# Sixteen-head attention before a transformer stream: one pipeline of four sequences in place of two passes of three stages

## The reference, cut to what matters

```python
x = x + attn_a(layernorm(x))          # changed part: x is 4 sequences x 512 tokens x 128, 16 heads of 8
x = x + ffn(layernorm(x))             # 2 layers of local attention + gated MLP
x = x + attn_b(layernorm(x))
x = x + ffn(layernorm(x))

def attn_a(x):
    q, k, v = split_heads(x @ w_qkv + b_qkv)                # (4, 16, 512, 8) each
    p = softmax(einsum('bhnd,bhmd->bhnm', q, k) * 8 ** -0.5)
    return merge_heads(einsum('bhnm,bhmd->bhnd', p, v)) @ w_proj + b_proj
```

## Time and profile before

| | |
|---|---|
| median of 3 runs | 1183.93 us (1179.61 to 1187.25) |
| profiled execution, its own time | 1180.76 us |
| its span, first to last instruction | 1179.0 us |
| busy in the span | TensorE 996.0, DVE 827.2, ACT 717.2, GpSimd 390.5 us |
| chain that ended last | TensorE 46%, DVE 13%, issue 4%, ACT 3%, GpSimd 2% |
| mean granted TensorE clock | 0.930 |

### The profile page before, as it was taken

How to read it: one execution, slowest core, us unless ns; L and a number is a source line. 1 busy time by engine, 2 the same in 40 slices (tenths; PEclk the granted TensorE clock), 3 DMA queues, 4 the chain that set the end, 5 groups by cost and what they waited for, 6 DMA issues and landing times.

```text
span 1179.0 us, 22117 instructions
## 1 busy us (share of the span) xinstructions
PE 996.0 (84%) x8272; PEld 595.4 (50%) x8272; DVE 827.2 (70%) x1381; ACT 717.2 (61%) x1500; POOL 390.5 (33%) x251
## 2 busy tenths in 40 slices
PE   5069997248997679999999979898989999999996
PEld 3023324112323466766766656555556666667662
DVE  3078823348863688888988877767777889888861
ACT  3027773106784477777677666656565776777762
POOL 5000005000000755445544434243434455445420
PEclk9589998659999699999999989999999999999998
DMA  2960000680000411011100101000000111011100
GB/s 56 132 122 10 1 1 19 102 106 8 2 1 1 101 27 24 20 24 24 29 20 19 28 8 26 6 19 15 19 15 19 25 24 29 16 24 37 34 10 18
DMA packets 38268, 36.01 MB, mean 31 GB/s; under 512 B 11478, under 2 KB 30224, under 8 KB 38160
## 3 DMA queue, kind: packets, MB, share of 16 engines
q1 hardware_dynamic: 34708, 31.46, 14.2%
q10 hardware_dynamic: 3456, 3.15, 1.2%
HBM read 15.41 MB, written 4.21 MB: 17 GB/s over the span
## 4 chain that ended last, share of the span: by engine, by line
PE 46%; DVE 13%; issue 4%; ACT 3%; POOL 2%; DVEq 0%; POOLq 0%
PE psum L1162 7%; PE psum L1134 5%; PE psum L1094 5%; PE psum L1073 4%; PE psum L1037 4%; PE psum L1170 4%; PE psum L1047 3%; PE psum L1083 3%; PE psum L1039 3%; PE psum L1038 3%; DVE f_NM L1424 3%; DVE f_A L1392 2%; DVE f_BS L1396 2%; DVE f_SS L1403 2%; DVE f_PT L1416 2%
## 5 line engine op out<-in xcount | busy, mean ns | idle before, releaser
L966 POOL TENSOR_TENSOR f_A<-f_A,f_BS 128x1024 f32<-128x1024 f32 x64 | 150.9, 2357 | 229.4 <-DVE f_BS L1396 229.3
L500 DVE TENSOR_REDUCE a_M<-psum 128x1 f32<-128x512 f32 x256 | 159.8, 683 | 60.1 <-PE psum L430 59.8
L430 PE MATMUL psum<-a_KS,a_QS 128*128 128x512 bf16 x256 | 102.6, 409 | 76.4 <-DMA a_KS<-minus_ones 72.6
L971 POOL TENSOR_TENSOR f_A<-f_A,f_RN 128x1024 f32<-128x1024 f32 x64 | 121.8, 1903 | 107.9 <-ACT f_RN L1282 107.2
L547 ACT ACTIVATE a_PT<-psum 128x1024 f32<-128x1024 f32 x128 | 126.4, 1018 | 50.9 <-PE psum L452 50.7
L1271 ACT ACTIVATE f_PW<-psum,f_NM 128x128 f32<-128x128 f32 x512 | 138.5, 381 | 14.5 <-DVE f_NM L1424 11.6
L1392 DVE TENSOR_TENSOR f_A<-psum,cos 128x512 f32<-128x512 f32 x128 | 87.7, 685 | 48.1 <-ACT f_SQ L1237 47.5
L1424 DVE TENSOR_REDUCE f_NM<-psum 128x4 f32<-128x512 f32 x128 | 81.9, 679 | 54.7 <-PE psum L1073 54.7
L1094 PE MATMUL psum<-f_VS,f_PT 128*64 128x65 f32 x1024 | 82.1, 229 | 38.6 <-DVE f_PT L1416 17.4
L1237 ACT ACTIVATE f_SQ<-psum 128x512 f32<-128x512 f32 x128 | 75.3, 607 | 61.4 <-PE psum L1039 57.1
L1094 PEld LDWEIGHTS psum<-f_VS,f_PT 128*64 128x64 f32 x1024 | 68.6, 140 | 71.6 <-issue 43.0
(11 more groups left out here) (173 smaller groups left out, 1971.8 us busy)
## 6 DMA issues: line engine op xcount, KB each, us to landing
f_VS<-f_V SPq DMA_DIRECT2D x112, 130.0 KB, 2.3
parts<-a_PRT ACTq DMA_DIRECT2D x24, 128.0 KB, 2.4
a_QS<-parts SPq DMA_DIRECT2D x8, 256.0 KB
a_KS<-parts SPq DMA_DIRECT2D x8, 256.0 KB
a_QS<-parts SPq DMA_DIRECT2D x4, 384.0 KB
a_KS<-parts SPq DMA_DIRECT2D x4, 384.0 KB
raw<-L_ffn_wqkv_dram SPq DMA_DIRECT2D x2, 768.0 KB, 6.5
a_XT<-L_attn_a_x_dram SPq DMA_DIRECT2D x4, 256.0 KB, 4.1
```

The source lines that it names most:

```text
L430: nc.tensor.matmul(psum[:, take("tile", 8 * unit + k), :], QS[:, n, h + k // 4, P * qt:P * qt + P], KS[:, n, h + k // 4, :], start=True, s ...
L500: nc.vector.tensor_reduce(M[:, u % 4, k // 4, k % 4:k % 4 + 1], psum[:, bank("tile", i), :], AX_X, ALU.max)\
L966: nc.gpsimd.tensor_tensor(A[:, k % 2, :, :], A[:, k % 2, :, :], BS[:, k % 2, :, :], ALU.add)\
L971: nc.gpsimd.tensor_tensor(x, x, RN[:, k % 2, :, None].to_broadcast([P, 2 * HW, DW]), ALU.mult)\
```

## The change

`attention_a` is written anew, for all four sequences, as one phase that runs by a table. Time is cut into slots; a slot is 128 queries of two heads. A quad is four heads and 8 slots, a sequence 32 slots, all 128. In a slot every engine first does `scores` of this slot, then `by_key` of the slot 14 earlier (`E_LAG`), then whatever `AROUND` puts at that place for some sequence. So TensorE's next sequence is normalized, projected and stacked, and the last one summed, projected and normalized, between slots of scores.

- [...] Four heads of a quad lie at partitions 0, 32, 64 and 96. TensorE builds the stacks itself, with a selection matrix (`SELECT`); ACT and DVE copy them from PSUM, DVE adding the -1. The parts' trip through DRAM and the clearing are gone; GpSimd splits q and k.
- A slot's two matmuls of `scores`, and the two of `by_key`, use different row groups of the array and write a pair of banks. Three pairs go round for both; two single banks for all else. DVE takes maxima of 1024 columns in one instruction (before, 512).
- Sums of a quad are made in two blocks of two key tiles, then turned to tokens and divided by quads (DVE, 128x16 and 128x128) instead of all heads at the end.
- Layer norm: variance by a matmul with ones, then Ln and Exp of 128x512 on ACT, product on GpSimd. No table loads but one.
- Layer 0's weights are split at slot 117 of the pipeline (ACT and GpSimd), the rotary tables made at slot 85 (GpSimd). The stream's wait for `zeroed` moves to the first tile's scores.

```diff
+QUADS = HA // 4
+SLOTS = 8 * QUADS
+E_LAG = 14
...
+AROUND = sorted([(-32, "turn_x", 0), (-29, "center_x", 0), (-27, "var_x", 0), (-21, "queries_keys", 0),
+                 (-16, "stack", 0), (-5, "stack", 1), (2, "values", 0), (4, "stack", 2), (8, "stack", 3),
+                 *((8 * quad + 9, "maxima", quad) for quad in range(QUADS)),
+                 *((8 * quad + 22, "sums", quad) for quad in range(QUADS)),
+                 *((8 * quad + 23, "sums_2", quad) for quad in range(QUADS)),
+                 *((8 * quad + 26, "turn_sums", quad) for quad in range(QUADS)),
+                 (51, "features", 0), (53, "project", 0), (56, "center_y", 0), (60, "var_y", 0)])
...
+    def pair(work, i):
+        return slice(2 * (pair_at[work, i] % 3), 2 * (pair_at[work, i] % 3) + 2)
+
+    def bank(work, i):
+        return 6 + at[work, i] % 2
...
+                        for j in range(4):
+                            sp.dma_start(QS[32 * j + ROWS_T:32 * j + ROWS_E, n % 2, quad, :].bitcast(F32),
+                                         MROW[j:j + 1, i % 2, :].bitcast(F32))\
+                              .then_inc(s(f"row_in{i % 2}"), 16)
...
+                    elif work == "stack":
+                        n, quad = i // QUADS, i % QUADS
+                        rows = slice(32 * quad, 32 * quad + 32)
...
+                        for w, kind in enumerate(("q_stack", "k_stack")):
+                            pe.wait_ge(s("low"), 2 * n + w + 1)
+                            dst = take(kind, i)
+                            nc.tensor.matmul(dst, SELECT[rows, 2 * w, :], QH[rows, w, :], start=True, stop=False)
+                            last = nc.tensor.matmul(dst, SELECT[rows, 2 * w + 1, :], QL[rows, w, :], start=False,
+                                                    stop=True)
+                            last.then_inc(s(kind), 1)
+                    elif work == "scores":
...
+                        dst = take_pair("scores", i)
+                        for h in range(2):
+                            rows = slice(32 * (2 * j + h), 32 * (2 * j + h) + ROWS_T)
+                            last = nc.tensor.matmul(dst[:, h, :], QS[rows, n % 2, quads % QUADS, P * t:P * t + P],
+                                                    KS[rows, n % 2, quads % QUADS, :], start=True, stop=True)
+                        last.then_inc(s("scored"), 1)
...
+                        if j == 0 and t == 0:
+                            pe.wait_ge(s(f"row_in{quads % 2}"), 64 * (quads // 2 + 1))
...
-                for i in range(3):
-                    cols = slice(T * i, T * i + T)
-                    pool.wait_ge(s("weights_high"), i + 1)
-                    nc.gpsimd.tensor_tensor(wqkv_l[:, 0, cols], g.raw[:, cols], wqkv_h[:, 0, cols].bitcast(F32),
-                                            ALU.subtract).then_inc(s("weights_low"), 1)
```

More of the change, by code:

```diff
@@ L16 @@
 T = 512
-NB = 2
 SEQS = 4
@@ L72, in constants @@
     col("ident")[:] = np.eye(P)
-    col("mean")[:] = 1.0 / P
+    quad, lane = r % 32, r[:, None] % 32
+    for i, parts in enumerate(((0, 1), (2,), (0, 2), (1,))):
+        for part in parts:
+            col("select")[r, P * i + 32 * (quad // DA) + DA * part + quad % DA] = 1
+    col("minus")[:] = np.where(lane == 3 * DA, -1.0, 0.0)
     col("center")[:] = np.eye(P) - 1.0 / P
@@ new lines, in slots_a @@
+def slots_a():
+    plan = []
+    for slot in range(AROUND[0][0], SEQS * SLOTS + AROUND[-1][0] + 1):
+        if 0 <= slot < SEQS * SLOTS:
+            plan.append(("scores", slot))
+        if 0 <= slot - E_LAG < SEQS * SLOTS:
+            plan.append(("by_key", slot - E_LAG))
+        for n in range(SEQS):
+            for at, work, quad in AROUND:
+                if SLOTS * n + at == slot:
+                    plan.append((work, QUADS * n + quad if work in PER_QUAD else n))
+    return plan
@@ new lines, in x_of @@
+                def x_of(n):
+                    return g.x_d[n:n + 1].rearrange("a (t p) d -> p (a t) d", p=P)
+                load(XT[:, 0, :, :], x_of(0), "x_loaded0")
+                load(g.const[:, :], a["const"][:, 0:KEPT], "const")
+                load(g.wa[:, :], a["L0_attn_a_w_qkv"], "wa")
+                for i in range(3):
+                    load(g.bqk[:, i:i + 1], g.column(a["L0_attn_a_b_qkv"][P * i:P * i + P]), "bias_in")
+                load(g.bpa[:, :], g.column(a["L0_attn_a_b_proj"]), "bias_in")
@@ L231, in _ @@
+                assert not todo
+                for name, n in (("tables", 1), ("const", 1), ("const_a", 1), ("wa", 1), ("bias_in", 5),
+                                ("weights", len(pieces))):
+                    sp.wait_ge(s(name), 16 * n)
             @block.gpsimd
@@ L626, in attention_a @@
-            s.close()
-def ln_buffers(alloc):
-    b = {k: alloc("ln_" + k, [P, NB, T]) for k in ("centered", "squared")}
-    b["recip"] = alloc("ln_recip", [P, NB, 4])
-    b["diag"] = alloc("ln_diag", [P, NB, 4, P])
-    return b
-def variance_pe(nc, out, squared, mean):
-    for t in range(4):
-        last = nc.tensor.matmul(out[:, t:t + 1], squared[:, P * t:P * t + P], mean, start=True, stop=True)
-    return last
-def diagonals(nc, g, out, recip):
-    return nc.vector.tensor_tensor(out, g.ident[:, None, :].to_broadcast([P, 4, P]),
-                                   recip[:, :, None].to_broadcast([P, 4, P]), ALU.mult)
@@ L698 @@
+        s.close()
 GROUP_TILES = SEQS * TILES
@@ L1226, in _ @@
                 nc.scalar.preload_act_table_set(EXP_AND_LN)
-                for i in range(3):
-                    cols = slice(T * i, T * i + T)
-                    nc.scalar.activation(wqkv_h[:, 0, cols], g.raw[:, cols], ACT.Copy).then_inc(s("weights_high"), 1)
                 for stage, i in engine_plan("ACT"):
```

787 lines of the change are left out of this document (374 added, 413 removed).

## The result

The changed kernel takes 1131.35 us (median of four runs, 1127.72 to 1133.68) against 1185.12 in the same comparison: a ratio of 0.955, interval 0.953 to 0.958. The forecast was 1101, range 1055 to 1145.

What follows compares the result with a forecast made beforehand. TensorE was taken to bound the main stage, with attention at 390.5 us of 1179. The new attention's 25 + 19 + 232 + 18 + 13 + 3 = 310 us meant 80 less than the profiled 1180.8: 1101 us, range 1055 to 1145.

Steps and rivals of the forecast that it cites:

- Head and tail: Stretch before the first scores, forecast at 25 us, and the last sequence's finish after the slots, forecast at 13 us.
- 114 full slots = 14.25 quads x 16.0: Slots with both scores and by-key: 16.0 us a quad, 232 us with late rows and weight splitting.
- Rival D: TensorE's clock falls because it stops briefly in every slot, making the kernel slower than before; chance 0.05.
- First 14 slots: 19: Opening slots, scores without by-key: 14 maxima of 1.14 us, two stacks and a centre on DVE, 19 us.
- by-key only: 18: Last 14 slots, without scores: 14 x 0.95 us, five blocks of sums partly ahead, a last-row wait, 18 us.
- TensorE is busy 84% with the mean clock at 0.93: Whole-span figures from the kernel before, offered as an argument against a falling clock.
- TensorE busy about 75%: Sign expected after the change, beside quads of 16 us in the middle of the pipeline.
- In a row 1.14, so DVE bounds a clean slot: Slot with nothing between pairs: lasts DVE's 1.14 us for a 1024-column maximum; the ring of banks needs 1.08.
- +3.1 for two blocks of sums: Per quad, two blocks of weighted sums, 2.06 us each on TensorE in neighbouring slots, add 3.1 us.
- A centre's +1.7: Layer norm's centring, twice a sequence: DVE waits for ACT's square and copies for 0.69 us; 1.7 us added each.
- Start of the stream 3.4: Until the stream's first projection: DVE's casts and subtractions take 2.8 us, 3.4 with the barrier; GpSimd's memsets run beside.
- C: Rival: pairs run one after the other, 1138 us, or rows come late in each quad, 1125 us; chance 0.20.

Runs made afterwards that it cites:

- f_full: Changed kernel plus, from slot 14 on, a filler matmul of constants, 128 rows and 512 columns long, ahead of each scores pair; 1130.3 us.
- f_short: Changed kernel plus, from slot 14 on, a filler matmul of constants, 128 rows but only 64 columns long, ahead of each scores pair; 1147.2 us.
- spreadq: Changed kernel with sums in four single-tile blocks, q and k in two neighbouring slots, and GpSimd's stream-start memsets behind DVE's casts; 1116.5 us.
- spread: Changed kernel with a quad's sums in four blocks of one key tile, in four neighbouring slots, instead of two blocks of two; 1110.5 us.
- red512: Changed kernel with DVE taking a slot's maxima in two instructions of 512 columns instead of one of 1024; 1129.0 us.
- cdefer: Changed kernel with DVE's copy of a layer norm's centred values behind the next slot's maximum instead of ahead of it; 1140.4 us.
- poolwait: Changed kernel with GpSimd's memsets at the start of the stream waiting until DVE has cast the first sequence; 1131.2 us.

## Why the prediction was right, and where it wasn't

The mechanism was right: the gain comes from prep, tail and start of the stream that no longer stand alone, and the main stage gives a part back. Head and tail were forecast to a microsecond (25 for 25.9, 13 for 12.5), and so were the prices: 0.23 for a pair, 1.2 for a maximum, 1.02 for an exponential. The time lies in the range, 2.7% above the forecast. That it is so near is in part luck, since two errors in the full slots have opposite signs.

- **The step that failed is the term "114 full slots = 14.25 quads x 16.0"**, which took TensorE's prices at clock 1.00 throughout. It measured 248.6 and not 232. In the full slots the clock was 0.77, so nearly half of the time was at the lower level, and a quad cost 17.5 in the mean. f_full and f_short show that it is the clock that costs. At the upper level a quad would have cost less than the 16.0: quads 5 and 6 take 15.05 and 13.87, quad 8 15.58, and quad 7 some 15.3 (f_full's 16.64 less the filler's 1.4), 14.9 in the mean. So the clock cost about 36 us (248.6 against 14.25 x 14.9), or 46 by 0.4 for each of the 116 us at the lower level, and the sum of delays was 1.1 us a quad too high, which hid 16 us of it. Both are estimates.
- Rival D named what happened, a clock that falls. Quads 5 and 6 price it: 0.42 and 0.37 us for each us at the lower level. Wrong was to take it only as slower than before and to give it 0.05: with the full slots at 0.77 the kernel is still 4.5% faster.
- **"First 14 slots: 19"** errs the same way: 24.7, at the lower level throughout by spreadq's trace; no run shows these slots at the upper level. Of **"by-key only: 18"** (20.5 at 0.83) spread shows it: up to the last by-key matmul 13.8 us at 1.00 and 17.8 at 0.81.
- **"TensorE is busy 84% with the mean clock at 0.93"**, the argument against D, was wrong to lean on busy time: f_short is busy 97% of its full slots at a clock of 0.76. The changed kernel's trace shows the clock swing between both levels, with quads at 1.00 next to quads at 0.71; what makes it swing, no run shows.
- **"TensorE busy about 75%"** as a sign was wrong too: it was busy 90% of the full slots, and 14.75 of 15.58 us in quad 8. A pair that stands alone counts 0.40 in the busy time where the sum took 0.23; for 16 pairs that is 2.7 us of the 2.8 between 14.75 and the counted 11.9.
- **"In a row 1.14, so DVE bounds a clean slot"**: true for the slots that last 1.13, but red512 shows that it decides nothing over a quad, where DVE waits for TensorE.
- **"+3.1 for two blocks of sums"**: at clock 1.00 the two slots took 2.66 and 2.34 us from one maximum to the next, against 2.85 and 2.52 counted. Four single blocks were counted at 2.8, and at equal clock the quads of spread bear that small gain out (0.2 against 0.3); what spread gained beyond it, the counting had no term for. A centre's +1.7 held 1.0 for DVE's wait, which measured 0.6; what a centre costs in all, cdefer can't tell, since its clock fell.
- **"Start of the stream 3.4"**: 5.9, since GpSimd's memsets "run beside" was wrong; poolwait gives the 2 us back at that place.
- Rivals: C's first form is out (pairs start 0.24 apart, two matmuls in each), and its second (late rows: 2.1 us in all). The total near C's 1138 would have been read as C without the trace.

## What to carry to other kernels

When stages that stood alone become one pipeline, count each engine's work per round first: here it was counted about as long as before, and all the gain was the ends. Then try the longest blocks of the fullest engine in smaller pieces: that was worth 21 us more, though the count of delays explains only some 4 of them and most of the rest came with the clock. And work out the sum at both of TensorE's clock levels, as ends of the range, instead of excluding the lower one by a high busy share: here 97% busy stood beside a clock of 0.76, and one and the same quad took 15.05 us at the upper level and 19.34 with half of its time at the lower. To price such a thing, compare rounds with the same content, not neighbours.

## What the runs showed of the hardware that was not expected

- Fillers in the same place left TensorE at different clocks: one of 128 rows and 64 columns at 0.76 in the full slots, one of 128 rows and 512 columns at 0.92 there, and at 0.97 with spread sums (in the profiled execution; the span's clock was lower in two of the other three). Pairs of 24 rows and 512 columns gave a clock of the span of 0.913 to 0.938, hardly more than without a filler (0.903 to 0.928).
- The pattern of levels repeated within an execution: quads 9 to 11 of the changed kernel took 19.33, 17.62 and 19.15 us, and quads 5 to 7, the same work one sequence earlier, 19.34, 17.64 and 19.15. It is not fixed by the work: in red512, alike but for the maxima, quad 5 was at 1.00 throughout.
- While a quad's content stayed the same, each us at the lower level cost about 0.4 us (19.34 against 15.05 with 10.2 us at that level, 17.64 against 13.87 with 10.2).
- A DVE cast of 64x4 took 1.9 us while GpSimd ran a memset of 64x2080, and 0.17 without it.
